# Gate products of a decoder kernel in four strips of 32 output partitions, summed by the product that turns them

## Chip, cores and metric

The kernel runs on one core of a Trainium2 chip. TensorE multiplies matrices (a float32 product is two records in a trace), VectorE, ScalarE and GpSimd work on elements, and SyncE issues most DMAs. The metric is the device time of one execution in microseconds, as the median over runs.

## What is computed

One decoder layer on x, 8 sequences of 256 tokens with 1024 features, all float32. It has three blocks, each behind a layernorm without weights, and each added to x:

```
x = x + attn(layernorm(x))               # 4 layers: scan over time, MLP 128 -> 512 -> 128
x = x + xattn(layernorm(x), ctx_4096)    # splits channels by top-k of ctx, gates both parts
x = x + ffn(layernorm(x))                # 8 experts, each token goes to its best two
...
gate_logits = jnp.einsum('bsh,he->bse', x, gate_w)        # x: (8, 256, 1024), gate_w: (1024, 8)
top_vals, top_idx = jax.lax.top_k(gate_logits, 2)
probs = jax.nn.softmax(top_vals, axis=-1)
expert_out = jnp.einsum('bsh,eho->bseo', x, expert_w)     # only of the chosen two in the kernel
```

The second block multiplies its input by a gate map, so the normed x before it (call it n1) times the map is what it adds. The change is about how `gate_logits` come about.

## The kernel before

The kernel is one program written out by hand: each engine has its own list, in program order, and waits on semaphores. No scheduler moves anything. It has these stages in time: the first block's four layers (to about 360 us); the stage in which x1 is made (`products`, `rows`), normed (`normed` on VectorE into `ring`), turned into feature-major tile T by TensorE (`turned`) and copied by ScalarE, while VectorE takes products and maxima over the channel groups (`crucial`, `maxima`, L1789 and L1798); the short serial stage of convolution and statistics (464 to 474 us: `band` products L1590 to L1595, filler products `keep_busy` L1603 of 512 bfloat16 columns that keep TensorE at work, sums over partitions L1607 and L1610, and a chain of small VectorE operations called `link`); the batch stage (474 to 530 us, 8 batches of 256 tokens); routing (to 561 us); and the loop over experts (L2099, from 563.64 us).

The logits of a token are found from two sums of products with gate_w, so that they don't wait for the whole second block. The first part, `first_part(c)` (c = 0 to 3, 512 tokens each), multiplies T before the gate map with the gate: eight products, one per block of 128 features, added up in one bank of the product memory, in its partitions 0 to 7. The second part, `second_part(b)` (b = 0 to 7, 256 tokens each), does the same with T after it was multiplied with the gate map. A sum is then copied by VectorE to `by_expert` (8 partitions wide; `first_sums` L1897, `second_sums` L1905) and turned to 128 tokens on partitions by 128x8 transposes (`first_turned` L1628, `second_turned` L1647), from where `known` and `logits` are made.

Where they stand in TensorE's list: `first_part(0)`, `first_part(1)` and the first half of `first_part(2)` behind the last turns of the x1 stage and ahead of the convolution; the second half of 2 and the first of 3 behind the statistics; the rest between `back(0)` and `first_turned(0)`. In the batch stage the order is `back(b)` (L1621: 16 transposes that turn the gated T back, for VectorE's `residual` L1877, which waits for each four), then `second_turned(b - 2)`, then `second_part(b)`; for b = 1, `first_turned(2)`, `first_turned(3)` and `second_part(0)` stand in the middle. VectorE's list for a batch is `residual(b)`, `behind(b - 1)` (L1891), `second_sums(b - 1)`, and the statistics of the new x. `back(b)` waits until `residual(b - 1)` has left its banks; `second_part(b)` waits for GpSimd's `gated_half` (L1472).

Of the kernel before, what the change touches and what calls it, by code (L numbers as in the profile page):

```python
# [8 lines left out]
U32 = mybir.dt.uint32  # L9
# [22 lines left out]
def crucial_count(c):  # L32
    f = int(LAMBDA * c // 1)
    return f + f % 2


def decoder_kernel(nc, x, ctx_map, w_in, b_in, ln1_w, ln1_b, phz_re, phz_im, lc_re, lc_im, sc_lin, ln2_w, ln2_b,
# [33 lines left out]
    with ctx:  # L71
# [26 lines left out]
        wout_t, bout_b = late[:, 0:D], late[:, D:2 * D]  # L98
        gate = sb("gate", [P, KD, E])
        convw = sb("convw", [P, 2 * TAPS])  # L100
# [47 lines left out]
        ld_misc = sem("ld_misc")  # L148
        ld_gate = sem("ld_gate")
        const_ready = sem("const_ready")  # L150
        set_pe = sem("set_pe")
# [230 lines left out]
        with nc.Block() as block:  # L382
            @block.sync
            def _(sp):
# [49 lines left out]
                context(3)  # L434
                sp.dma_start(gate[:, :, :], gate_w.rearrange("(k p) e -> p k e", p=P)).then_inc(ld_gate, 16)
                weights(2)
# [12 lines left out]
            def _(pool):  # L449
# [73 lines left out]
                def last_threshold(b):  # L523
# [12 lines left out]
                    chained(t2_set)  # L536

                g.memset(ident[:, :], 0.0).then_inc(const_ready, 1)
                g.memset(ones[:, :], 1.0).then_inc(const_ready, 1)
# [768 lines left out]
        pooled = ewide[:, 0:4 * KD * B].rearrange("p (m i k b) -> p m i k b", m=2, i=2, k=KD)  # L1308
        logits = sb("logits", [P, NT, E])
        totals = logits[:, :, :].rearrange("p t e -> p (t e)")[:, 0:KD * B].rearrange("p (k b) -> p k b", k=KD)  # L1310
# [12 lines left out]
        def pool_at(i, n):  # L1323
            b, h = divmod(n, CT)
            return pooled[:, 0, i, h * KU:(h + 1) * KU, b]

        def first_part(pe, c, first, last):

            if first == 0:
                pe.wait_ge(t_set, (c + 1) * KD * GROUP // S)  # L1330
                pe.wait_ge(x1_done, 2 * (NT - 2) + c + 1)
            for k in range(first, last):
                mm = nc.tensor.matmul(bank[P1_SUMS[c]][0:E, :], gate[:, k, :], T[:, k, c * GROUP:(c + 1) * GROUP], start=(k == 0), stop=(k == KD - 1))
            if last == KD:
                mm.then_inc(p1_mm, 1)
# [22 lines left out]
        std = in_late(NT)  # L1358
        g_part = in_late(E)
        known = in_late(NT, E)  # L1360
        shift = in_late(NT, E)
# [95 lines left out]
        P1 = N // GROUP  # L1457
        by_expert = [fin[0:E, u, :] for u in range(2)]

# [29 lines left out]
        col_s = [sb(f"col_s{u}", [P, QK], U32) for u in range(IN_FLIGHT)]  # L1489
        col_d = [sb(f"col_d{u}", [P, 1], U32) for u in range(IN_FLIGHT)]  # L1490
        col_p = [sb(f"col_p{u}", [P, 1]) for u in range(IN_FLIGHT)]
        xg_in = [sem(f"xg_in{u}") for u in range(IN_FLIGHT)]
# [10 lines left out]
        with nc.Block() as block:  # L1503
# [56 lines left out]
            def _(pe):  # L1560
# [63 lines left out]
                def first_turned(c):  # L1624
                    pe.wait_ge(p1_cp, c + 1)
                    for u in range(GROUP // P):
                        t = c * (GROUP // P) + u
                        mm = nc.tensor.transpose(bank[P1_BANK][:, t * E:(t + 1) * E], by_expert[c % 2][:, u * P:(u + 1) * P], ident[0:E, 0:E])  # L1628
                    mm.then_inc(p1_tp, 1)

                def second_part(b):

                    if b == 0:
                        pe.wait_ge(p1_cp, P1)
                    if b >= 2:
                        pe.wait_ge(p1_cp, P1 + b - 1)
                    for n in range(2):
                        wait_gated(pe, b, n)
                    for k in range(KD):
                        mm = nc.tensor.matmul(bank[P2_SUMS[b % 2]][0:E, 0:S], gate[:, k, :], T[:, k, b * S:(b + 1) * S], start=(k == 0), stop=(k == KD - 1))  # L1640
                    mm.then_inc(p1_mm, 1)

                def second_turned(b):
                    pe.wait_ge(p1_cp, P1 + b + 1)
                    for h in range(CT):
                        t = CT * b + h
                        mm = nc.tensor.transpose(bank[P2_BANK][:, t * E:(t + 1) * E], by_expert[b % 2][:, h * P:(h + 1) * P], ident[0:E, 0:E])  # L1647
                    mm.then_inc(l_mm, 1)
# [131 lines left out]
            def _(dve):  # L1780
# [68 lines left out]
                link(v.tensor_scalar(z[:, :, :], z[:, :, :], 0.0, None, ALU.max))  # L1849
                link(v.tensor_reduce(g_part, gate[:, :, :].rearrange("p k e -> p e k"), AX.X, ALU.add))  # L1850
                dve.wait_ge(g_act, 1)
# [41 lines left out]
                def first_sums(c):  # L1893
                    if c >= 2:
                        hold(dve, p1_tp, c - 1)
                    hold(dve, p1_mm, c + 1)
                    v.tensor_copy(by_expert[c % 2], bank[P1_SUMS[c]][0:E, :]).then_inc(p1_cp, 1)  # L1897

                def second_sums(b):
                    if b < 2:  # L1900
                        hold(dve, p1_tp, P1)
                    else:
                        hold(dve, l_mm, b - 1)
                    hold(dve, p1_mm, P1 + b + 1)
                    v.tensor_copy(by_expert[b % 2][:, 0:S], bank[P2_SUMS[b % 2]][0:E, 0:S]).then_inc(p1_cp, 1)  # L1905

# [315 lines left out]
```

## Time and profile before

| | us |
|---|---|
| median of 3 runs | 1089.44 (1087.9 to 1091.88) |
| the profiled execution | 1089.82 |
| its span, first to last instruction | 1087.9 |
| TensorE busy with products | 995.9 (92%) |
| VectorE busy | 538.7 (50%) |
| ScalarE, GpSimd busy | 383.5, 453.9 |
| mean granted TensorE clock | 0.955 of full speed |

Busy shares are means over stages with different bounds: the last 47% of the span belong to the expert products alone, and what lies before them must be read by stage. All times below count from the span's start.

### The profile page before, as it was taken

Reading aid. Unit: us, or ns where it says so; the run is one execution under the profiler, and the core shown is the slowest. Engines: PE = TensorE matmul, PEld = TensorE weight load, DVE = VectorE, ACT = ScalarE, POOL = GpSimd, SP = SyncE. Lnnn points to the kernel's source line nnn. Section 1 sums busy time; section 2 is a strip of 40 time slices with the busy share of each in tenths; the row PEclk is TensorE's granted clock in tenths of the full one; section 3 lists DMA queues with packets and bytes.
Section 4 is the critical chain, followed back from the end, with each engine's and each line's share of the span. In section 5 each row is a group of like instructions: output and inputs, shape, how many; then the busy total and the mean of one; then the engine's idle time right before and its main releaser. Section 6 shows DMA issues by size and latency. Waiting matters only on the chain. (4 is left out here: it accounts for less than half of the span.)

```text
span 1087.9 us, 13206 instructions
## 1 busy us (share of the span) xinstructions
PE 995.9 (92%) x3505; PEld 525.7 (48%) x3512; DVE 538.7 (50%) x1547; ACT 383.5 (35%) x1032; POOL 453.9 (42%) x567
## 2 busy tenths in 40 slices
PE   6888989999989799899469999999999999999995
PEld 5777555565555454245234444444444444444442
DVE  5645878999978889979952111111211111111111
ACT  2344868888865278668410000000000000000000
POOL 4823655665552010048244334333334444444441
PEclk9888989999989899899759999999999999999998
DMA  7320120110001330007758463737337364373332
GB/s 298 129 98 2 50 88 1 59 40 2 1 1 54 144 113 1 2 20 286 295 208 259 103 203 77 231 77 226 82 82 226 77 204 104 77 231 77 77 77 39
DMA packets 38461, 120.24 MB, mean 111 GB/s; under 512 B 6220, under 2 KB 9351, under 8 KB 38408
## 3 DMA queue, kind: packets, MB, share of 16 engines
q1 hardware_dynamic: 25592, 79.77, 19.8%
q0 software_dynamic: 12816, 39.86, 16.7%
q8 instruction: 21, 0.34, 0.1%
q14 instruction: 32, 0.26, 0.1%
HBM read 82.91 MB, written 36.70 MB: 110 GB/s over the span
## 5 line engine op out<-in xcount | busy, mean ns | idle before, releaser
L2099 PE MATMUL bank<-T,X 128*128 x1184 | 511.1, 595 | 3.7 <-issue 3.7
L2099 PEld LDWEIGHTS bank<-T,X 128*128 128x128 f32 x1184 | 225.9, 191 | 288.3 <-issue 288.3
L2144 DVE TENSOR_SCALAR X<-bank,col_p 128x512 f32<-128x512 f32 x37 | 27.8, 751 | 397.1 <-PE bank L2099 397.1
L2117 ACT ACTIVATE X<-bank,col_p 128x512 f32<-128x512 f32 x37 | 25.4, 687 | 495.8 <-PE bank L2099 469.7
L2062 POOL DMA_INDIRECT out_dram<-X,col_d x37 | 60.0, 1622 | 264.3 <-DVE X L2144 248.1
L2053 POOL DMA_INDIRECT X<-x_nrm,col_s x152 | 145.5, 957 | 50.8 <-issue 46.2
L850 ACT ACTIVATE M<-X,T 128x256 bf16<-128x256 f32 x152 | 75.0, 500 | 0.0
L490 POOL TENSOR_TENSOR rs<-ve,neg_half 128x4 f32<-128x4 f32 x36 | 43.7, 1214 | 57.9 <-DVE ve L978 57.9
L665 PE MATMUL bank<-nat,T 128*128 128x512 f32 x128 | 63.2, 614 | 2.5 <-ACT X L838 1.4
L1501 DVE STREAM_TRANSPOSE X<-X 128x1024 f32<-128x1024 f32 x39 | 48.4, 1240 | 26.3 <-DMA X<-x_nrm,col_s 12.7
L673 PE MATMUL bank<-X,T 128*128 128x512 f32 x128 | 60.6, 602 | 0.0
L607 PE MATMUL bank<-ident,rs 128*128 128x128 f32 x320 | 44.5, 285 | 16.4 <-POOL rs L490 14.2
L607 PEld LDWEIGHTS bank<-ident,rs 128*128 128x128 f32 x320 | 41.7, 195 | 36.5 <-POOL rs L490 23.0
L235 POOL TENSOR_TENSOR late<-late,neg_half 128x1 f32<-128x1 f32 x32 | 17.7, 556 | 93.3 <-DVE late L231 93.0
L838 ACT ACTIVATE X<-bank,T 128x512 f32<-128x512 f32 x64 | 43.5, 686 | 19.4 <-PE bank L665 17.9
L1009 DVE MAX8 T<-T 128x8 f32<-128x256 f32 x128 | 44.8, 412 | 0.1
L984 DVE TENSOR_TENSOR nat<-H,bank 128x512 f32<-128x512 f32 x36 | 24.5, 682 | 38.9 <-PE bank L607 38.5
L969 DVE TENSOR_TENSOR_SCAN X<-layer_par,X 128x256 f32<-128x256 f32 x64 | 42.7, 730 | 2.1 <-POOL X L494 2.0
L481 POOL TENSOR_TENSOR T<-T 128x8 f32<-128x8 f32 x88 | 38.2, 434 | 7.9 <-POOL T L481 1.4
L665 PEld LDWEIGHTS bank<-nat,T 128*128 128x128 f32 x128 | 21.7, 191 | 36.4 <-ACT X L838 21.8
L602 PEld LDWEIGHTS bank<-inv_col,nat 128*128 128x128 f32 x288 | 37.2, 202 | 2.6 <-ACT nat L825 2.2
L602 PE MATMUL bank<-inv_col,nat 128*128 128x1 f32 x288 | 37.1, 250 | 0.8 <-ACT nat L825 0.8
(341 smaller groups left out, 1426.6 us busy)
## 6 DMA issues: line engine op xcount, KB each, us to landing
T<-in_L_ffn_expert_w_dram SPq DMA_DIRECT2D x8, 4096.0 KB, 17.6
out_dram<-X SPq DMA_DIRECT2D x17, 512.0 KB
M<-in_x_dram SPq DMA_DIRECT2D x16, 512.0 KB, 7.2
X<-in_x_dram SPq DMA_DIRECT2D x16, 512.0 KB, 5.9
x_nrm<-H SPq DMA_DIRECT2D x16, 512.0 KB, 3.4
T<-in_ctx_dram SPq DMA_DIRECT2D x9, 512.0 KB, 3.7
X<-x_nrm,col_s POOLq DMA_INDIRECT x152
X<-in_ctx_dram SPq DMA_DIRECT2D x4, 512.0 KB, 7.0
```

What stands on the lines that cost most here:

```text
L490: g.tensor_tensor(rs[:, v % CH, :], ve[:, v % CH, :], neg_half[:, 0:TPC], ALU.pow).then_inc(done, 1)
L602: mm = nc.tensor.matmul(var_at(v, first)[:, i:i + 1], chunk(sq, v)[:, i * P:(i + 1) * P], inv_col[:, :], start=True, stop=True)
L607: mm = nc.tensor.matmul(bank[to][:, i * P:(i + 1) * P], rs[:, v % CH, i:i + 1].to_broadcast([P, P]), ident[:, :], start=True, stop=True)
L665: nc.tensor.matmul(bank[HD[t % 2]][:, :], w1s[v // CH % 2][:, t * P:(t + 1) * P], chunk(yn, v), start=True, stop=True).then_inc(hid_mm, 1)
L673: mm = nc.tensor.matmul(h_bank(v), w2c[v // CH % 2][:, t, :], hid[:, v % 2, t, :], start=False, stop=(t == FT - 1), skip_group_check=True)
L838: a.activation(hid[:, v % 2, t, :], bank[HD[t % 2]][:, :], ACT.Silu, bias=b1f[v // CH % 2][:, t:t + 1]).then_inc(hid_act, 1)
L850: a.activation(out_, tile_y(b, i), ACT.Sign, bias=at[b % 2][:, i:i + 1], accum_out=sums[b % 2][:, i:i + 1]).then_inc(done, 1)
L1009: v_.max(top16[b % 2][:, h * HT + i, r * 8:(r + 1) * 8], w[:, h, i, :]).then_inc(round_max, 1)
L1501: nc.vector.transpose(xgt_blocks[u], xg_blocks[u]).then_inc(xg_tp, 1)
L2053: g.indirect_dma_start(out=xg[u][:, c * QD:(c + 1) * QD], out_offset=None, in_=x_quarters, in_offset=bass.IndirectOffsetOnAxis(ap=col_s[u] ...
L2062: g.indirect_dma_start(out=out[:, :], out_offset=bass.IndirectOffsetOnAxis(ap=col_d[u][:, 0:1], axis=0), in_=yv[u], in_offset=None, comput ...
L2099: mm = nc.tensor.matmul(bank[2 * u + n][:, :], xgt[u][:, k, :], Tf[:, ds(odd * D + (k * N + n * BANK), BANK)], start=(k == 0), stop=(k == ...
```

## The change

The tile `gate` gets 32 columns per feature block in place of 8; the 24 new ones are zeroed by GpSimd at the start, and SyncE's load of the gate waits for that. Product k of a sum writes the partitions 32(k mod 4) to 32(k mod 4) + 31, so that four partial sums, of two feature blocks each, stand in four strips of a bank. The first four products of a sum start a strip, the last four close one. VectorE copies all 128 partitions. The turn becomes a float32 product: the copied block is the weight, and `sum_e`, a 128x8 matrix with a one in row 32j + e, column e, for j = 0 to 3, is multiplied with it; so it turns and adds the four strips at once. VectorE makes `sum_e` by one more reduction (of the identity) in the link chain ahead of L1850.

To make room, `logits` moves into the tile `center`, and `col_d` and `col_p` into the tiles `mv` and `ve`, which have no other use by then.

No instruction changes its place on any engine: GpSimd has one more (the zeroing, its first), VectorE one more (the reduction), and TensorE the same products in the same order.

```diff
-        gate = sb("gate", [P, KD, E])
+        gate = sb("gate", [P, KD, GROUP_E])
...
-                sp.dma_start(gate[:, :, :], gate_w.rearrange("(k p) e -> p k e", p=P)).then_inc(ld_gate, 16)
+                sp.wait_ge(gate_clear, 1)
+                sp.dma_start(gate[:, :, 0:E], gate_w.rearrange("(k p) e -> p k e", p=P)).then_inc(ld_gate, 16)
...
+                g.memset(gate[:, :, :], 0.0).then_inc(gate_clear, 1)
...
-        logits = sb("logits", [P, NT, E])
+        logits = center[:, :].rearrange("p (t e) -> p t e", e=E)
...
+        def of_group(sums, k):
+
+            j = k % GROUPS
+            return sums[j * GROUP_E:(j + 1) * GROUP_E, :]
...
-                mm = nc.tensor.matmul(bank[P1_SUMS[c]][0:E, :], gate[:, k, :], T[:, k, c * GROUP:(c + 1) * GROUP], start=(k == 0), stop=(k == KD - 1))
+                mm = nc.tensor.matmul(of_group(bank[P1_SUMS[c]], k), gate[:, k, :], T[:, k, c * GROUP:(c + 1) * GROUP], start=(k < GROUPS), stop=(k >= KD - GROUPS))
...
-        by_expert = [fin[0:E, u, :] for u in range(2)]
+        by_expert = [fin[:, u, :] for u in range(2)]
...
-        col_d = [sb(f"col_d{u}", [P, 1], U32) for u in range(IN_FLIGHT)]
-        col_p = [sb(f"col_p{u}", [P, 1]) for u in range(IN_FLIGHT)]
+        col_d = [mv[:, u, 0:1].bitcast(U32) for u in range(IN_FLIGHT)]
+        col_p = [ve[:, u, 0:1] for u in range(IN_FLIGHT)]
...
-                        mm = nc.tensor.transpose(bank[P1_BANK][:, t * E:(t + 1) * E], by_expert[c % 2][:, u * P:(u + 1) * P], ident[0:E, 0:E])
+                        mm = nc.tensor.matmul(bank[P1_BANK][:, t * E:(t + 1) * E], by_expert[c % 2][:, u * P:(u + 1) * P], sum_e[:, :], start=True, stop=True)
...
-                        mm = nc.tensor.matmul(bank[P2_SUMS[b % 2]][0:E, 0:S], gate[:, k, :], T[:, k, b * S:(b + 1) * S], start=(k == 0), stop=(k == KD - 1))
+                        mm = nc.tensor.matmul(of_group(bank[P2_SUMS[b % 2]], k)[:, 0:S], gate[:, k, :], T[:, k, b * S:(b + 1) * S], start=(k < GROUPS), stop=(k >= KD - GROUPS))
...
+                v.tensor_reduce(sum_e[:, :], ident[:, :].rearrange("p (j e) -> p e j", j=GROUPS)[:, 0:E, :], AX.X, ALU.add)
...
-                    v.tensor_copy(by_expert[c % 2], bank[P1_SUMS[c]][0:E, :]).then_inc(p1_cp, 1)
+                    v.tensor_copy(by_expert[c % 2], bank[P1_SUMS[c]][:, :]).then_inc(p1_cp, 1)
```

`GROUPS` is 4 and `GROUP_E` 32. The turn in `second_turned` and the copy in `second_sums` change in the same way.

## Rows read from the trace of the kernel before

**Rows 1.** The page's costliest groups: busy, mean ns | idle before, releaser

```profile
L2099 PE MATMUL bank<-T,X 128*128 x1184 | 511.1, 595 | 3.7 <-issue 3.7
```

**Rows 2.** Instructions on the tile gate: ns min/median/max, first and last start

```profile
L1640 PE MATMUL bank<-T,gate x128: 379/379/383, 486.1 to 526.8; 128*8 128x256 f32 x128
...
L1333 PE MATMUL bank<-T,gate x64: 592/592/1061, 442.7 to 482.2; 128*8 128x512 f32 x64
```

**Rows 3.** TensorE's timeline, 440 to 470 us: start, us, instruction [idle before <-releaser]

```profile
440.80 1.97 PE L1569 MATMUL bank<-ident,nat 128*128 128x128 f32 x8 [4.58 <-DVE nat L1806]
...
447.99 1.09 PE L1569 MATMUL bank<-ident,nat 128*128 128x128 f32 x8
...
453.56 10.47 PE L1333 MATMUL bank<-T,gate 128*8 128x512 f32 x24
464.87 0.71 PE L1590 MATMUL bank<-ewide,band 128*128 128x128 f32 x4 [0.84 <-DVE ewide L1826]
...
466.93 0.39 PE L1595 MATMUL bank<-ewide,band 128*128 128x56 f32 x2
467.15 1.46 PE L1603 MATMUL bank<-ones,ident 128*128 128x512 bf16 x6
468.44 0.28 PE L1607 MATMUL bank<-late,ones 128*128 128x2 f32 x2
...
470.03 0.38 PE L1610 MATMUL bank<-late,ones 128*128 128x2 f32 x2
```

**Rows 4.** VectorE's timeline in convolution and statistics, 464 to 473 us

```profile
464.52 0.30 DVE L1826 TENSOR_SCALAR ewide<-ewide 128x64 f32<-128x64 f32 x2
467.35 0.29 DVE L1837 COPY late<-bank 128x128 f32<-128x128 f32 x1 [2.53 <-PE bank L1595]
...
468.84 0.16 DVE L1840 TENSOR_SCALAR late<-bank 128x2 f32<-128x2 f32 x1 [0.88 <-PE bank L1607]
...
472.94 0.22 DVE L1853 TENSOR_TENSOR late<-late 128x64 f32<-128x64 f32 x1
```

**Rows 5.** Busy by stretch: PE, PEld, DVE, ACT, POOL, clock, DMA, GB/s

```profile
436.00:436.50 0.50, 0.22 (x2) 0.00 (x0) 0.50 (x5) 0.50 (x4) 0.00 (x0) 1.00 0.00 0
...
439.00:439.50 0.50, 0.00 (x0) 0.00 (x0) 0.50 (x3) 0.00 (x0) 0.00 (x0) 0.94 0.00 0
...
446.00:446.50 0.50, 0.50 (x2) 0.14 (x1) 0.50 (x2) 0.50 (x5) 0.00 (x0) 0.73 0.00 0
```

**Rows 6.** TensorE's timeline in the batch stage, 483 to 527 us

```profile
483.32 0.39 PE L1654 MATMUL bank<-late,ones 128*128 128x8 f32 x2
...
485.44 0.71 PE L1628 MATMUL bank<-ident,fin 8*128 8x8 f32 x8
486.08 7.07 PE L1640 MATMUL bank<-T,gate 128*8 128x256 f32 x32
493.08 1.97 PE L1621 MATMUL bank<-ident,T 128*128 128x128 f32 x16
494.98 0.29 PE L1647 MATMUL bank<-ident,fin 8*128 8x8 f32 x2
...
523.58 3.62 PE L1640 MATMUL bank<-T,gate 128*8 128x256 f32 x16
```

**Rows 7.** VectorE's timeline in the batch stage, 489 to 528 us

```profile
489.85 0.41 DVE L1905 COPY fin<-bank 8x256 f32<-8x256 f32 x1 [1.53 <-PE bank L1640]
...
501.42 2.48 DVE L1877 TENSOR_TENSOR X<-X,bank 128x512 f32<-128x512 f32 x4 [0.18 <-DVE late L1934]
...
507.96 2.48 DVE L1877 TENSOR_TENSOR X<-X,bank 128x512 f32<-128x512 f32 x4
...
527.53 0.40 DVE L1905 COPY fin<-bank 8x256 f32<-8x256 f32 x1
```

**Rows 8.** The timeline of the first microseconds: GpSimd's zeroing and TensorE's first product

```profile
0.99 0.43 POOL L540 MEMSET ewide<- 128x390 f32 x1
...
6.49 0.33 PE L744 MATMUL bank<-ident,T 59*128 59x59 f32 x1 [6.49 <-DMA T<-in_L_attn_lnl_b_dram]
```

More of the change, by code:

```diff
@@ L34, in crucial_count @@
     return f + f % 2
+GROUPS = 4
+GROUP_E = 128 // GROUPS
 def decoder_kernel(nc, x, ctx_map, w_in, b_in, ln1_w, ln1_b, phz_re, phz_im, lc_re, lc_im, sc_lin, ln2_w, ln2_b,
@@ L149, in decoder_kernel @@
         ld_gate = sem("ld_gate")
+        gate_clear = sem("gate_clear")
         const_ready = sem("const_ready")
@@ L1359, in decoder_kernel @@
         g_part = in_late(E)
+        sum_e = in_late(E)
         known = in_late(NT, E)
@@ L1646, in second_turned @@
                         t = CT * b + h
-                        mm = nc.tensor.transpose(bank[P2_BANK][:, t * E:(t + 1) * E], by_expert[b % 2][:, h * P:(h + 1) * P], ident[0:E, 0:E])
+                        mm = nc.tensor.matmul(bank[P2_BANK][:, t * E:(t + 1) * E], by_expert[b % 2][:, h * P:(h + 1) * P], sum_e[:, :], start=True, stop=True)
                     mm.then_inc(l_mm, 1)
@@ L1849, in _ @@
                 link(v.tensor_scalar(z[:, :, :], z[:, :, :], 0.0, None, ALU.max))
-                link(v.tensor_reduce(g_part, gate[:, :, :].rearrange("p k e -> p e k"), AX.X, ALU.add))
+                v.tensor_reduce(sum_e[:, :], ident[:, :].rearrange("p (j e) -> p e j", j=GROUPS)[:, 0:E, :], AX.X, ALU.add)
+                link(v.tensor_reduce(g_part, gate[:, :, 0:E].rearrange("p k e -> p e k"), AX.X, ALU.add))
                 dve.wait_ge(g_act, 1)
@@ L1904, in second_sums @@
                     hold(dve, p1_mm, P1 + b + 1)
-                    v.tensor_copy(by_expert[b % 2][:, 0:S], bank[P2_SUMS[b % 2]][0:E, 0:S]).then_inc(p1_cp, 1)
+                    v.tensor_copy(by_expert[b % 2][:, 0:S], bank[P2_SUMS[b % 2]][:, 0:S]).then_inc(p1_cp, 1)
                 for k in range(KU):
```

## The prediction

> **What bounds the kernel now.** I first read the chain that ended last and the table of costly groups. The routed expert products (L2099) are 1184 matmul records, 511.1 us of a span of 1087.9 [rows 1]. They start at 563.64 us and the change does not touch them, so what it can win or lose must lie before that moment. I then looked for the gate products by line: L1333 (first part, 32 products of 128x512 in 64 records) and L1640 (second part, 64 products of 128x256 in 128 records) [rows 2]. A float32 product is two records. Their starts are the measure of their cost, since a record's own length has a tail that overlaps the next. At L1333 24 records took 10.47 us, 0.43 us a record, 0.86 a product; at L1640 32 took 7.07 us, 0.22 a record, 0.43 a product [rows 3, 6]. So the gate products hold TensorE for 32 x 0.86 + 64 x 0.43 = 55 us.
>
> The third view, the timeline of two engines side by side, tells what those 55 us are worth. Before 464.87 us TensorE runs L1333 while VectorE does the channel sums, and the next TensorE step, the convolution L1590, starts when VectorE has done L1826 (464.52 + 0.30 = 464.82), 0.84 us after TensorE fell idle [rows 3, 4]. TensorE is no bound there. In the batch stage (478 to 528 us) TensorE looks full: per batch 16 back-turns (1.90 us from 493.08 to 494.98), two logit turns (0.2) and a second part (3.62 with its tail), 5.7 us together. But VectorE takes 6.54 us a batch (501.42 to 507.96) and does not wait [rows 6, 7]. There VectorE is the bound and TensorE is ahead of it. The one place where VectorE waits for a gate product is the copy of the second part of batch 0: 1.53 us at 489.85 [rows 7]. It is the only stall in the trace that faster gate products can take away.
>
> **What the change does to the products.** The eight products of a sum now write four strips of 32 partitions in turn (k modulo 4), and each still is two records. The trace of before has no two products in different strips, so their overlap has to be bounded. At one end nothing overlaps: 0.86 us a 512-column product. At the other end four run at once: 0.22. I take a middle: the second record of a product needs the strip of its first, so it starts 0.43 us after it; the first record of the next product, in another strip, can run beside it; if records start in program order, as every row here shows them, a stream then moves one product per record time. That is 0.43 us per 512-column product and 0.22 per 256-column one, half of before.
>
> The Trainium skill ("TensorE: Matmul & The Clock Gate", Part 3: Packing small matmuls) says that products in different column strips run at the same time and that matmuls start and end in program order. No row here shows the first; the second agrees with every row. The same part says that weight loads pass running matmuls only where the row group differs, which is not so for column strips, and by it little overlap would be left: that is the third case below.
>
> **Convolution and statistics (the largest term).** L1333 there is 12 products, now 10.47 us from 453.56. At half the time they end at about 453.56 + 12 x 0.43 + 0.43 = 459.1. The convolution still waits for VectorE until 464.87, so TensorE idles 5.7 us instead of 0.84. What an idle stretch does to its clock is in the trace: its last work before 440.80 ended at 436.2, and the granted clock was down to half in the half microsecond from 439.0 [rows 5]: 3.2 us later. It is at half (1.2 instead of 2.4 GHz) at 440.80, where eight transposes took 1.97 us against 1.09 at the full clock [rows 3], and comes back at 446.25 (0.73 in the half from 446.0), 5.4 us after work resumed. So after the change the clock falls at about 462.3, the convolution starts at half clock, and full clock returns near 464.87 + 5.4 = 470.3. The 20 convolution records took 2.28 us (464.87 to 467.15); at half clock about 4.5, to 469.4. Behind them stand six filler products of 512 bf16 columns, 1.29 us to L1607 (468.44); of these 0.9 us run at half clock and the rest at full: they end at about 471.1 and L1607 is 2.7 us late. VectorE sat idle for each of these steps (2.53 us before L1837, 0.88 before L1840) [rows 4], so the delay is on the path. The second filler group then runs at full clock and adds nothing. Term: **+2.7 us**. Its ends: 0 where the clock holds; 4.7 where the clock stays at half through both fillers (2.2 + 1.3 + 1.2).
>
> **The stall at 489.85.** The turn of a sum was a transpose, one record; it is now a float32 product with the strip-adding matrix, two records. The nearest product of that shape, L1654, took 0.39 us for its two records, and 16 records with as many weight columns took 1.97 in a row, so 0.1 us for each record more [rows 6]. The turns of the third and fourth 512-column sums (8 records, 0.71 us at 485.44) get 8 more: 0.8 us. The second part of batch 0 then starts at 486.9 instead of 486.08, takes 8 x 0.22 + 0.22 = 1.9 instead of 3.45, and ends near 488.9 instead of 489.6. The copy goes 0.7 us earlier: **-0.7 us**. Ends: -1.5 (the whole stall, if four overlap), +0.8 (no overlap). Behind that, VectorE's 6.54 us a batch stay the bound: TensorE needs 1.97 + 0.5 + 1.9 = 4.4.
>
> **Small edits.** The new reduction of the identity on VectorE sits in the serial gate chain between L1849 and L1853 and is read from 32 numbers a partition; small VectorE operations here take 0.15 to 0.22, the last of them L1853 [rows 4]: **+0.15 us** (0 if wholly under the sigmoid, 0.3 at most). The zeroing of the gate tile is 256 numbers a partition, under the 0.43 us of L540 with 390; it delays GpSimd's constants by 0.3 us at 1 us, and TensorE's first step waits for a DMA until 6.49 [rows 8]: 0, and 0.3 without that cover. SyncE's new wait for it is passed a hundred microseconds later. The copies read 128 partitions instead of 8 at equal width; 8x256 took 0.41, and four operations of 128x512 from the same kind of tile 2.48, 0.6 each [rows 7], so a width of 256 on all partitions costs no more than that: 0. The new homes of logits, col_d and col_p move nothing. The gate load is one DMA that lands hundreds of microseconds early: 0. All else keeps its order.
>
> **Sum.** 2.7 - 0.7 + 0.15 = +2.15 us on the profiled execution's 1089.8 (span 1087.9 and 1.9 around it): 1092.0. The median of the runs is 0.4 under that execution, so 1091.6. All that follows is against the median, 1089.4.
>
> **The rivals.**
> *The clock holds.* The overlap is as above, but TensorE's idle stretch doesn't meet the throttle, or VectorE's steps before it end sooner: -0.7 + 0.15, 1088.9. For it: the stretch is only 2.5 us longer than the 3.2 after which it fell. Against it: it did fall there.
> *No overlap: the change doesn't do what it says.* The products take what they took, and only the longer turns remain. VectorE's copy waits 0.8 us longer at 489.85. Then TensorE, at 5.7 + 0.2 a batch, stays under 6.54 at first, but the last three batches of VectorE come closer, and its last copy at 527.53 follows TensorE's last second part (from 523.58 for 3.62 us) closely [rows 6, 7]. That part would end 0.8 + 6 x 0.22 = 2.1 us later, the copy about 1.9 later: 1089.4 + 1.9 + 0.15 = 1091.4. No clock is lost.
> *All four strips at once.* The products take a quarter. The stall goes wholly (-1.5), TensorE idles from 456.8 to 464.87, so the half clock is certain: +2.7. Together +1.35: 1090.8. The Trainium skill ("TensorEngine Tiling (Array Packing)", Overview) gives up to 4x for 32 columns; no run here shows it.
> *Slower beyond doubt: half clock in the batch stage.* If four overlap, TensorE works 1.97 + 0.5 + 1.0 = 3.5 of 6.54 us a batch and the gap is 3.1 us, near the 3.2 after which the clock fell. At half clock a batch is 7 to 9 us of TensorE and it becomes the bound; without a gap it then wins the clock back after some 5.4 us, so about every second of six batches loses 2.3 us: +7 on top of the forecast's 2.15, 1098.5. It decides from a gap of about 3.2 us on; at my rate the gap is 2.1, which is against it.
>
> **How the numbers follow.** Forecast (pairs overlap, cold convolution) 0.42; clock holds 0.18; no overlap 0.20; four at once 0.13; half clock in the batches 0.07. The predicted time is 1091.6. The first four cases lie between 1088.9 and 1091.6; with the bounds of the clock term (4.7 instead of 2.7: 1093.6), the third bound of the stall, and the spread of the runs before (1087.9 to 1091.9) the range is 1087.5 to 1094.5. Half a percent is 5.4 us, about what a measurement of this kernel can tell from no change: to a time under 1084.0 none of these cases leads, and 0.02 stands for what I don't see; over 1094.9 the last case and a little of the clock's tail, 0.08; within, 0.90.
>
> **What would show it.** In the profile after: L1333's and L1640's records in starts per product (0.43 and 0.22 right, 0.86 and 0.43 no overlap, less for four); TensorE idle for 5 us before the convolution and a granted clock of 0.50 at 465 us; the convolution's 20 records over 4 us; VectorE's waits for them up by 2 to 3 us; the wait before the batch 0 copy at about 0.8; VectorE still at 6.5 us a batch with the clock at 1.00; the expert loop at 511 us. The forecast fails if the products don't overlap, if the granted clock stays at 1.00 at 465 us, or if VectorE waits for TensorE in the batches.

## The result, and the profile of the changed kernel

The changed kernel takes 1093.2 us (median of 20 runs, 1089.14 to 1097.17) against 1089.09 (20 runs, 1087.08 to 1092.27). The ratio is 1.0031, with a 95% interval of 1.0019 to 1.0043: slower by 0.3%, less than the half percent that the prediction names, with a median 1.6 us above the forecast. Its profiled span is 1091.9 us (before 1087.9) and its mean granted clock 0.936 (before 0.955).

The expert loop is the same, one line of the page's costliest groups, to be read beside [rows 1]:

```profile
L2113 PE MATMUL bank<-T,X 128*128 x1184 | 511.0, 595 | 4.0 <-issue 4.0
```

So the 4.0 us lie before it. TensorE's timeline of the changed kernel from the last first-part products ahead of the convolution to the second part of batch 0 (start, us, instruction, idle before and its releaser) answers to [rows 3, 6]; lines have moved by 12 to 14, so L1345 is the old L1333, L1603 the old L1590, L1653 the old L1640, L1641 the old L1628, and L1634 the old L1621:

```profile
453.99 4.25 PE L1345 MATMUL bank<-T,gate 128*32 128x512 f32 x24
465.76 1.23 PE L1603 MATMUL bank<-ewide,band 128*128 128x128 f32 x4 [7.52 <-DVE ewide L1839]
...
470.07 2.77 PE L1616 MATMUL bank<-ones,ident 128*128 128x512 bf16 x6
472.63 0.43 PE L1620 MATMUL bank<-late,ones 128*128 128x2 f32 x2
...
474.76 0.28 PE L1623 MATMUL bank<-late,ones 128*128 128x2 f32 x2
474.97 1.92 PE L1345 MATMUL bank<-T,gate 128*32 128x512 f32 x16
...
485.32 1.95 PE L1641 MATMUL bank<-late,fin 128*128 128x8 f32 x16
...
487.36 3.33 PE L1634 MATMUL bank<-ident,T 128*128 128x128 f32 x16
490.48 2.17 PE L1641 MATMUL bank<-late,fin 128*128 128x8 f32 x16
492.57 1.93 PE L1653 MATMUL bank<-T,gate 128*32 128x256 f32 x32
```

Sixteen records of L1345 take 1.92 us at the full clock, 0.12 each, 0.24 a product, where [rows 3] had 0.86. The second part's 32 records take 1.93 instead of 7.07 [rows 6]. From the first start of L1653 to the start of the work behind it the 32 records hold TensorE for 1.87 us (492.57 to 494.44) where they held it for 7.00: by a factor of 3.7 less, close to a quarter and not half. (The 24 records from 453.99 took 4.25 us, more than 24 times 0.12, because the granted clock was at half from 453.6 to 457.0.) In front of the convolution TensorE is now idle for 7.52 us instead of 0.84.

VectorE's timeline of the changed kernel in the same stretch and three batches on, which answers to [rows 4, 7]:

```profile
465.41 0.29 DVE L1839 TENSOR_SCALAR ewide<-ewide 128x64 f32<-128x64 f32 x2
470.32 0.29 DVE L1850 COPY late<-bank 128x128 f32<-128x128 f32 x1 [4.61 <-PE bank L1608]
...
473.17 0.16 DVE L1853 TENSOR_SCALAR late<-bank 128x2 f32<-128x2 f32 x1 [2.24 <-PE bank L1620]
...
475.15 0.16 DVE L1858 TENSOR_SCALAR late<-bank 128x2 f32<-128x2 f32 x1 [0.85 <-PE bank L1623]
...
477.58 0.22 DVE L1867 TENSOR_TENSOR late<-late 128x64 f32<-128x64 f32 x1
...
493.82 0.42 DVE L1919 COPY fin<-bank 128x256 f32<-128x256 f32 x1 [0.84 <-PE bank L1653]
...
505.50 2.48 DVE L1891 TENSOR_TENSOR X<-X,bank 128x512 f32<-128x512 f32 x4 [0.18 <-DVE late L1948]
...
512.06 2.48 DVE L1891 TENSOR_TENSOR X<-X,bank 128x512 f32<-128x512 f32 x4
```

The three waits for TensorE in convolution and statistics have grown from 2.53, 0.88 and 0.55 to 4.61, 2.24 and 0.85. The third one before stood in this line:

```profile
470.52 0.16 DVE L1845 TENSOR_SCALAR late<-bank 128x2 f32<-128x2 f32 x1 [0.55 <-PE bank L1610]
```

The reason stands in the view by stretch (busy of PE, PEld, DVE, ACT, POOL, then the granted clock, DMA share, GB/s), first of the kernel before, then of the changed kernel:

```profile
467.00:474.00 7.00, 7.00 (x28) 2.57 (x28) 3.92 (x15) 1.01 (x3) 0.70 (x1) 1.00 0.00 0
```

```profile
464.00:466.00 2.00, 0.24 (x1) 0.24 (x2) 1.41 (x9) 1.08 (x1) 0.00 (x0) 0.50 0.00 0
...
472.00:474.00 2.00, 2.00 (x7) 1.03 (x6) 0.74 (x3) 0.00 (x0) 0.00 (x0) 0.50 0.00 0
474.00:476.00 2.00, 2.00 (x18) 0.99 (x20) 0.45 (x2) 0.00 (x0) 0.61 (x1) 0.98 0.00 0
...
505.00:511.00 6.00, 4.66 (x25) 4.44 (x29) 5.61 (x14) 4.55 (x7) 5.85 (x6) 0.50 0.60 235
```

Both of the chip's levels are there: 0.50 is 1.2 GHz, 1.00 is 2.4. In the kernel before, the same stage ran at 1.00 throughout. In the changed one TensorE's last product ended at 458.24 and the granted clock fell at 460.4. The convolution, the first sum over partitions and most of the fillers now run at half clock, and the clock comes back at 474.1 us, 8.3 us after TensorE took up work. It also fell for times in the batch stage: from 480.9 to 484.3 and from 487.8 to 491.2, which bears on the stall of batch 0 (below), and again from 504.8 on, as the last row shows, where it cost nothing.

Taken stage by stage between VectorE's own marks, the 4.0 us come together like this:

| stretch | before | after | difference |
|---|---|---|---|
| start of span to convolution input (L1826, now L1839) | 464.52 | 465.41 | +0.89 |
| to the copy of its result | 2.83 | 4.91 | +2.08 |
| to the mean | 1.49 | 2.85 | +1.36 |
| to the variance | 1.68 | 1.98 | +0.30 |
| to the difference of the averages (L1853, now L1867) | 2.42 | 2.43 | 0.0 |
| to the copy of batch 0 | 16.91 | 16.24 | -0.67 |
| to the start of the loop | 73.79 | 73.92 | +0.13 |
| loop and end | 524.3 | 524.2 | -0.1 |

The first row is not the change's. In twelve profiled runs of this study, the place where the convolution's input is ready lies between 462.4 and 467.2 us (5.8 us of added copies taken off in one), in kernels with strips in the first part (462.9, 464.3, 465.2, 465.4, 467.0, 467.2) as in those without (462.4, 462.5, 464.5, 465.0, 465.4, 466.7). One place where the two profiles part is in the first block: near 100 us the clock was at half for some 3 us in the kernel before (from 98.1) and for some 7 in the changed one (from 105.4), and TensorE's work is 1 us later behind it. Differences of a microsecond between two profiles are therefore read by stage, and those between kernels from the medians.

### The profile page after: what moved, and what is told of

Same layout as the page of the kernel before. It is cut to its first block and busy times, and to the rows that moved or that the text cites. A ratio compares the mean times of both kernels' runs of the same rounds, so it can differ in the third digit from the quotient of the medians.

```text
span 1091.9 us, 13272 instructions
## 1 busy us (share of the span) xinstructions
PE 974.4 (89%) x3537; PEld 531.9 (49%) x3544; DVE 539.2 (49%) x1548; ACT 383.7 (35%) x1032; POOL 455.2 (42%) x568
## 5 line engine op out<-in xcount | busy, mean ns | idle before, releaser
L2158 DVE TENSOR_SCALAR X<-bank,ve 128x512 f32<-128x512 f32 x37 | 27.8, 751 | 394.8 <-PE bank L2113 394.8
L2131 ACT ACTIVATE X<-bank,ve 128x512 f32<-128x512 f32 x37 | 25.4, 687 | 495.4 <-PE bank L2113 495.4
L2076 POOL DMA_INDIRECT out_dram<-X,mv x37 | 60.0, 1622 | 263.9 <-DVE X L2158 247.7
```

The costliest lines, as they stand in the source:

```text
L2076: g.indirect_dma_start(out=out[:, :], out_offset=bass.IndirectOffsetOnAxis(ap=col_d[u][:, 0:1], axis=0), in_=yv[u], in_offset=None, comput ...
```

## The experiments

The theory after the result: (A) the first part's saving is worth nothing, since VectorE bounds TensorE there, and its idle stretch costs the clock in the serial stage, some 3.7 us; (B) the second part's saving is worth up to the 1.53 us stall of batch 0, and the longer turns take back about half. The rivals: the strips cost something by themselves, or the wider gate and the longer turns do; and for the overlap: pairs, or all four strips.

**e1_fill: filler products ahead of the convolution.** The changed kernel with `keep_busy` defined earlier and

```diff
+                pe.wait_ge(t_set, KD * B)
+                keep_busy(7, 24)
```

in TensorE's list between the first-part products and the convolution.

> The changed kernel with 24 filler products of 512 bfloat16 columns on TensorE between the last first-part product and the convolution (5.2 us at the full clock), nothing else. Clock theory (the loss is the convolution and statistics at half clock, behind an idle stretch of 7.5 us that the faster products left): the granted clock is 1.00 at the convolution, its 20 records take 2.3 us again instead of 4.3, VectorE's two waits fall from 4.6 and 2.2 us to 2.5 and 0.9, and the time falls by 3.4 to 3.8 us from the changed kernel's, to a ratio of 0.999 to 1.000 to the kernel before. Rival (the longer turns and wider copies in the batches cost it): the time stays at 1.003.

Measured: 1089.94 us (12 runs) against 1090.17, ratio 1.0001 (0.9987 to 1.0014). The loss of 0.31% is gone from the medians. But the profiled execution missed part of what was expected. TensorE's timeline of e1_fill:

```profile
455.62 5.35 PE L1606 MATMUL bank<-ones,ident 128*128 128x512 bf16 x24
463.21 0.71 PE L1612 MATMUL bank<-ewide,band 128*128 128x128 f32 x4 [2.23 <-DVE ewide L1841]
...
464.99 0.63 PE L1617 MATMUL bank<-ewide,band 128*128 128x56 f32 x2
```

The fillers ended 2.23 us early, and from 464.7 us on the clock was at half in this execution (0.63 instead of 0.39 us for two records of 56 columns), in the middle of the work. So the clock fell here behind a gap of 2.2 us, too. VectorE's three waits were 3.35, 2.25 and 1.43 us, 3.07 more than before, so this execution kept most of the 3.75 us that it should have won back, against the expected waits of 2.5 and 0.9. That its time (1090.5 us) lies near that of the kernel before comes from an early start: its convolution's input was ready at 462.9. The medians agree with (A), but this profile does not show it, and e1 alone is no proof.

**e8_fill_both: enough fillers, at both gaps.** As e1_fill, with

```diff
-                keep_busy(7, 24)
+                keep_busy(7, 34)
...
+                keep_busy(7, 16)
```

the second group behind the products at 472.8 us, ahead of `back(0)`.

> The changed kernel with 34 filler products ahead of the convolution (7.3 us at full clock, up to VectorE's last sums) and 16 in the idle stretch of 3.9 us between the statistics and the first back-turns. Clock theory: granted clock 1.00 from 457 us to the batches, VectorE's waits in convolution and statistics 2.5 to 2.9, 0.9 and 0.5 us, and the stall at the copy of batch 0's second part smaller than 0.8; ratio 0.998 to 0.999. Rival (the fillers themselves delay the path): waits over 3 us at a clock of 1.00.

Measured: 1089.43 us (11 runs) against 1090.33, ratio 0.9984 (0.9969 to 0.9999). VectorE's timeline first and then TensorE's, of e8_fill_both:

```profile
469.83 0.29 DVE L1853 COPY late<-bank 128x128 f32<-128x128 f32 x1 [2.53 <-PE bank L1617]
...
471.32 0.16 DVE L1856 TENSOR_SCALAR late<-bank 128x2 f32<-128x2 f32 x1 [0.88 <-PE bank L1622]
...
491.65 0.43 DVE L1922 COPY fin<-bank 128x256 f32<-128x256 f32 x1 [0.82 <-PE bank L1656]
```

```profile
459.81 7.51 PE L1606 MATMUL bank<-ones,ident 128*128 128x512 bf16 x34
...
487.65 1.95 PE L1644 MATMUL bank<-late,fin 128*128 128x8 f32 x16 [1.90 <-DVE fin L1914]
489.54 3.61 PE L1656 MATMUL bank<-T,gate 128*32 128x256 f32 x32
```

With TensorE at work the waits are 2.53 and 0.88 to the hundredth as in [rows 4], the third is 0.55, and the granted clock was 1.00 from 458.9 to 489.5. The whole +3.75 is the clock's. The stall of batch 0 stayed at 0.82, where less had been expected: the turns had to wait for VectorE's copy of the sums, then took 1.95 us, and the products of batch 0 behind them ran at half clock (32 records in 3.61 us instead of 1.93), which is as much again as the stall.

**e5_idle: the same gap without any strip.** The kernel before, with work put into VectorE's list ahead of the averages:

```diff
+                for i in range(8):
+                    v.tensor_copy(ring[1], X[:, 0, :]).then_inc(extra, 1)
+                    dve.wait_ge(extra, i + 1)
```

> The kernel before, with eight copies of 1024 columns on VectorE (about 7 us of empty work) between its last channel maxima and the averages, so that TensorE idles some 8 us ahead of the convolution with no strips anywhere. Clock theory: the convolution takes 4.3 us instead of 2.3, VectorE's waits there grow to 4.6 and 2.2 us as in the changed kernel, and the time grows by the copies plus 3.5 to 3.8 us. Rival (strips or the 32-column gate slow the convolution): the waits stay at 2.5 and 0.9 us and only the copies are added.

Measured: 1100.52 us (4 runs) against 1090.33, ratio 1.0076 (1.0053 to 1.0099). TensorE and VectorE of e5_idle:

```profile
471.17 1.22 PE L1591 MATMUL bank<-ewide,band 128*128 128x128 f32 x4 [6.82 <-DVE ewide L1830]
```

```profile
475.72 0.29 DVE L1841 COPY late<-bank 128x128 f32<-128x128 f32 x1 [4.61 <-PE bank L1596]
...
478.58 0.16 DVE L1844 TENSOR_SCALAR late<-bank 128x2 f32<-128x2 f32 x1 [2.25 <-PE bank L1608]
...
481.08 0.16 DVE L1849 TENSOR_SCALAR late<-bank 128x2 f32<-128x2 f32 x1 [1.38 <-PE bank L1611]
```

The copies took 5.8 us (not the 7 I had counted on) and the gap was 6.8 (not 8). The waits of 4.61 and 2.25 are those of the changed kernel, in a kernel whose products are the old ones; the third is 1.38, since the clock came back only at 480.6, 9.4 us after work resumed. The half clock follows the gap, not the strips. From the convolution's input to the difference of the averages the stage is 4.3 us longer, and with 5.8 us of copies that is 10.1, what the medians say (10.2; the ratio of four runs says 8.3, with an interval from 5.8 to 10.8).

**e2_second_only: strips in the second part alone.** The first part goes to one strip of 32 partitions, and its turn is a product with the first 32 rows of `sum_e`:

```diff
-                mm = nc.tensor.matmul(of_group(bank[P1_SUMS[c]], k), gate[:, k, :], T[:, k, c * GROUP:(c + 1) * GROUP], start=(k < GROUPS), stop=(k >= KD - GROUPS))
+                mm = nc.tensor.matmul(bank[P1_SUMS[c]][0:GROUP_E, :], gate[:, k, :], T[:, k, c * GROUP:(c + 1) * GROUP], start=(k == 0), stop=(k == KD - 1))
```

> Strips in the second part alone; the first part sums in one strip of 32 and is turned by a product over 32 partitions. Clock theory: the first part again fills TensorE up to the convolution, so no loss there (VectorE's waits 2.5 and 0.9 us), and the second part's gain at the one stall stays (1.5 us down to 0.8 or less): ratio 0.999 to 1.000. Rival (strips cost time in themselves, by switching, or the turns cost it): slower than before, 1.001 to 1.003.

Measured: 1089.04 us (12 runs) against 1090.17, ratio 0.9999 (0.9984 to 1.0014). TensorE and VectorE of e2_second_only:

```profile
484.73 1.95 PE L1641 MATMUL bank<-late,fin 32*128 32x8 f32 x16
486.61 1.93 PE L1653 MATMUL bank<-T,gate 128*32 128x256 f32 x32
```

```profile
487.86 0.42 DVE L1919 COPY fin<-bank 128x256 f32<-128x256 f32 x1 [1.49 <-PE bank L1653]
```

No clock is lost, since TensorE has its old amount of work ahead of the convolution: VectorE's waits there are 2.53, 0.88 and 0.55. But the stall is 1.49, as long as before and not 0.8 as expected: what the second part wins, the turns take away. There are two groups of them ahead of that copy, each 16 records in 1.95 us where 8 transposes took 0.66 and 0.71 ([rows 6] has the second). I had priced only one of the groups.

**e3_first_only: strips in the first part alone.** The second part in one strip, by the same kind of edit.

> Strips in the first part alone; the second part in one strip, turned by a product. Clock theory: the convolution is at half clock again, plus 3.5 to 4 us, and the stall at the copy of batch 0's second part is not shortened but lengthened, 1.5 to over 2 us: ratio 1.003 to 1.005. Rival (the batch stage carries the loss): 1.000 to 1.001.

Measured: 1096.45 us (6 runs), ratio 1.0060 (1.0043 to 1.0078). VectorE of e3_first_only:

```profile
470.07 0.29 DVE L1850 COPY late<-bank 128x128 f32<-128x128 f32 x1 [4.61 <-PE bank L1608]
...
495.31 0.41 DVE L1919 COPY fin<-bank 32x256 f32<-32x256 f32 x1 [2.50 <-PE bank L1653]
```

The clock is lost and the stall grows by 0.97. The time is above the expected 1.003 to 1.005: VectorE's last copy of the batch stage waits 1.53 us for TensorE, which had not been counted. With 3.8 from the clock these make 6.3 us, as the medians do. The longer turns are in this run too; against e4_one_strip (next), which has the turns and no strips, strips in the first part shorten the stall from 4.03 to 2.50 and lose 3.8 us by the clock, so by themselves they cost more than they bring.

**e4_one_strip: no strips at all, all else of the change.** Both parts in one strip: the gate's width, the wider copies' place, the turns as products and the new reduction remain.

> No strips: both parts sum in one strip of 32 columns, everything else of the change stays (wider gate tile, zeroing, product turns, extra reduction, moved tiles). It is the case of no overlap of the prediction, which gave +1.9 and +0.15 us: ratio 1.0015 to 1.002, with the last copies of VectorE waiting for TensorE about 2 us. Clock theory: no clock loss at the convolution. If the gate width of 32 costs TensorE time, a product of 512 columns takes over 0.86 us.

Measured: 1093.81 us (12 runs) against 1090.17, ratio 1.0034 (1.0021 to 1.0048). TensorE and VectorE of e4_one_strip:

```profile
468.16 7.05 PE L1345 MATMUL bank<-T,gate 128*32 128x512 f32 x16
...
486.46 7.09 PE L1653 MATMUL bank<-T,gate 128*32 128x256 f32 x32
```

```profile
490.25 0.41 DVE L1919 COPY fin<-bank 32x256 f32<-32x256 f32 x1 [4.03 <-PE bank L1653]
...
529.74 0.41 DVE L1919 COPY fin<-bank 32x256 f32<-32x256 f32 x1 [1.53 <-PE bank L1653]
```

With 32 columns of weights instead of 8 a product takes as long as before (7.05 us for 16 records of 512 columns, 7.03 before; 7.09 for 32 of 256, 7.07 in [rows 6]), so the width is free. The clock holds in the convolution. The stall is 4.03, 2.5 more than 1.53: two groups of turns, each 1.25 longer. Another 1.53 us appear as a wait before the last copy of the batch stage. This is the prediction's second rival carried out, and it costs 3.7 us by the ratio (3.6 between the medians), not 2.05 (1.9 and 0.15).

**e6_two_strips: two strips instead of four.** One run.

```diff
-            j = k % GROUPS
+            j = k % 2
```

with start and stop to match, and copies and turns of 64 partitions.

> The changed kernel with two strips (k modulo 2) in place of four. If a product in another strip starts beside the one before at no cost, the products of 512 columns take 0.43 us each at full clock, 0.22 for 256 columns, twice what four strips take. If overlap was limited by the pair of records of a product, as the prediction had it, two strips would take the same as four.

Measured: 1092.77 us. TensorE of e6_two_strips:

```profile
473.88 3.63 PE L1345 MATMUL bank<-T,gate 128*32 128x512 f32 x16
...
490.92 3.65 PE L1653 MATMUL bank<-T,gate 128*32 128x256 f32 x32
```

Two strips take 3.63 of one strip's 7.05 us, four 1.92: the time goes down nearly in proportion to the strips, and two strips don't take the same as four.

**e7_adjacent: four strips, neighbouring products in the same one.** One run.

```diff
-            j = k % GROUPS
+            j = k // 2
```

> The changed kernel with the blocks dealt to the strips in neighbours (blocks 0 and 1 to strip 0, 2 and 3 to strip 1, and so on) in place of one after the other in turn; the same products, turns and sum. It tells whether four strips overlap because neighbouring products lie in different strips, or because later products may pass earlier ones. If a product waits for the one ahead of it in its own strip and the products behind it wait too (order kept), then only products of different pairs overlap, and of every two products about one is hidden: the eight gate products of the first part take between 0.43 and 0.65 us each, against 0.24 in the changed kernel and 0.87 with one strip, so they are no quicker than with two strips. If products may pass one another, 0.22 to 0.24 us a product, as in the changed kernel. Convolution and averages run at the half clock in both cases; the span lies between 1088 and 1094 us.

Measured: 1093.83 us. TensorE of e7_adjacent:

```profile
476.88 1.94 PE L1345 MATMUL bank<-T,gate 128*32 128x512 f32 x16
```

As fast as with alternating strips. If a product held up all that stand behind it until its strip is free, this would have taken two to three times as long. In this kernel as in the changed one the view by tenths of a microsecond has four of these records in progress at a time (eight where one four follows another). Which of two explanations holds, that records of another strip start ahead of a waiting one or that some queue behind the start takes them in, these rows don't tell, because they don't name the strip of a record.

The profile shows one thing more. The work is the same as in the changed kernel, but VectorE doesn't wait at the copy of batch 0:

```profile
494.94 0.42 DVE L1919 COPY fin<-bank 128x256 f32<-128x256 f32 x1
```

Here the granted clock was 1.00 from 486.4 on, and the stretch from the difference of the averages to this copy is 15.45 us (16.24 in the changed kernel, 16.91 before). In the changed kernel's profile the clock was at half from 487.8 to 491.2. So the 0.84 us that were left of the stall there come from the clock, too, and not from the turns alone.

**e9_mixed and e10_mixed_again: the version the runs point to.** Strips in the second part alone, as e2_second_only, but the first part exactly as in the kernel before: 8 partitions, and transposes of one record.

```diff
-                        mm = nc.tensor.matmul(bank[P1_BANK][:, t * E:(t + 1) * E], by_expert[c % 2][0:GROUP_E, u * P:(u + 1) * P], sum_e[0:GROUP_E, :], start=True, stop=True)
+                        mm = nc.tensor.transpose(bank[P1_BANK][:, t * E:(t + 1) * E], by_expert[c % 2][0:E, u * P:(u + 1) * P], ident[0:E, 0:E])
```

> Strips in the second part alone, and the first part exactly as in the kernel before: 8 partitions wide, turned by one-record transposes. If the longer turns ate the gain of the second part in the run with strips in the second part alone, that gain comes back here: the second part of batch 0 ends 2.4 us earlier than before, so VectorE's 1.5 us wait at its copy is gone, the convolution is untouched, ratio 0.9985 to 0.999. Rival (the stall has another cause, such as the gated tiles of GpSimd): the wait stays near 1.5 and the ratio at 1.000.

Measured: 1087.43 us (12 runs, 1084.58 to 1089.58) against 1090.33 (23 runs), ratio 0.9965 (0.9952 to 0.9978). TensorE and VectorE of e9_mixed:

```profile
487.60 0.72 PE L1641 MATMUL bank<-ident,fin 8*128 8x8 f32 x8
488.24 1.93 PE L1653 MATMUL bank<-T,gate 128*32 128x256 f32 x32
```

```profile
475.10 0.22 DVE L1867 TENSOR_TENSOR late<-late 128x64 f32<-128x64 f32 x1
...
490.41 0.40 DVE L1919 COPY fin<-bank 128x256 f32<-128x256 f32 x1
```

The wait before the copy is gone, and the stretch from the difference of the averages to it is 15.3 us instead of 16.91: -1.6. The time is lower than the expected ratio of 0.9985 to 0.999; 1.3 us of the medians' 2.9 were unexplained, so the same kernel was run once more.

> The kernel of e9_mixed word for word, once more. Its profile accounts for 1.5 us less than before from the convolution on, its times for 2.9. If the stages tell the whole, the ratio comes out at 0.9986, with an interval that holds it; if the stages before the convolution are really shorter in most executions, the ratio is again near 0.9965 and a second profile may begin the convolution before 464.5 us, where the kernel before did (e9_mixed: 466.7). In both cases no wait before the batch 0 copy, 1.5 to 1.7 us less from the difference of the averages to that copy, and convolution and averages as in the kernel before.

Measured: 1086.21 us (12 runs) against 1089.48 (17 runs), ratio 0.9970 (0.9957 to 0.9983), so the 0.9986 lies outside the interval. The stretch is 15.31 again, the convolution's input ready at 465.42, no earlier than before, so in the profile the stages ahead are not the rest either. It is in the loop: the pages of the two give

```profile
L2113 PE MATMUL bank<-T,X 128*128 x1184 | 510.1, 594 | 4.4 <-issue 4.4
```

and 510.0 for the same records, where [rows 1] has 511.1. The view by stretch of the kernel before, whose loop begins at 563.64, and then of e9_mixed, whose loop begins at 564.34:

```profile
568.00:570.00 2.00, 2.00 (x5) 0.94 (x4) 0.00 (x0) 0.00 (x0) 1.40 (x2) 0.71 1.03 404
```

```profile
566.00:568.00 2.00, 2.00 (x4) 0.81 (x3) 0.00 (x0) 0.00 (x0) 1.39 (x3) 0.55 1.01 391
568.00:570.00 2.00, 2.00 (x7) 0.81 (x6) 0.00 (x0) 0.00 (x0) 1.59 (x2) 1.00 1.00 389
```

The loop of e9_mixed runs at half clock for its first 3.5 us, that of e10_mixed_again for 3.3, that of the kernel before (563.64 to 569.2) for 5.5. A microsecond less at half clock is worth half a microsecond here: 2.0 and 2.2 us less, and a loop shorter by 1.0 and 1.1. With -1.6 that makes -2.6 to -2.7, near the medians' -2.9 and -3.3. Why the clock is back sooner in both profiles isn't shown. It is no mark of this version: the loop took 509.8 us in e7_adjacent, where the clock was back after 3.0 us, and 510.7 to 511.3 in the other profiles. So 1.6 us are shown to be the edit's; the other microsecond was there in both profiles and has no known cause.

## Why the prediction was right or wrong

The sign was right and the time within the range, 1.6 us above the forecast. Three steps were not right: how products in strips overlap, when the clock comes back, and what the turns cost. The first and the third cancelled in the stall, and that was luck.

**How products in strips overlap: wrong.** The step that failed is "if records start in program order [...] a stream then moves one product per record time". Which of its two conditions failed, the order of the starts or a record's wait for the one ahead of it in its strip, is not shown. Four strips gave 0.24 us a product and not 0.43 (the changed kernel), two gave 0.45 (e6_two_strips), and the deal among the strips doesn't matter (e7_adjacent: 0.24). The case "all four strips at once" holds, which I had at 0.13. It is the one that the Trainium skill ("TensorEngine Tiling (Array Packing)", Overview) states, up to 4x for 32 columns: here 0.87 to 0.24 us. The other rule of the Trainium skill that I had weighed, from "TensorE: Matmul & The Clock Gate", Part 3: Packing small matmuls, that weight loads pass running products only where the row group differs, did not limit anything: all records here use all rows, and their time fell to little over a quarter.

**Convolution and statistics: mechanism right, term too small.** +2.7 was forecast, +3.75 measured, inside the stated ends of 0 and 4.7. The convolution's 20 records took 4.31 us (465.76 to 470.07) for the 4.5 I had. What was off is the clock's return: I took over 5.4 us from the one precedent in the trace and had it back at 470.3, ahead of most of the fillers. It came back at 474.1, 8.3 us after work resumed, and in e5_idle some 9.4 us after. So the first fillers cost 1.3 more instead of 0.4 and the second group another 0.4. One precedent is no constant. The same holds for the fall: the prediction had 3.2 us from the end of work to the half clock, and here it was 2.2 (458.24 to 460.4). e8_fill_both shows that nothing but the clock is in this term.

**Stall of batch 0: right size by luck.** -0.7 forecast, -0.67 measured. The products saved more than I had: from 4.03 in e4_one_strip to 1.49 in e2_second_only, which is 2.54 instead of 1.55. The turns cost more. I had priced one of the two groups ahead of that copy, at 0.8, with 0.1 us for a record where the row that I read gives 0.12 (1.97 for 16); both groups count, at 1.25 each at full clock. Two groups at 1.25 on top of 1.53 make 4.03, which is e4_one_strip's stall. In the changed kernel the first part's last products, ahead of the first turns, are quicker too, and the half clock takes part of that back, which the forecast had at nothing here. Counted by starts on TensorE, which doesn't pause between the back-turns of batch 0 and that copy:

| step | before | after | difference |
|---|---|---|---|
| difference of the averages to the back-turns of batch 0 | 4.37 | 3.20 | -1.17 |
| these back-turns | 1.89 | 3.55 | +1.66 |
| last products of the first part | 3.53 | 0.99 | -2.54 |
| first group of turns | 0.59 | 1.81 | +1.22 |
| to the end of the back-turns of batch 1 | 2.12 | 3.35 | +1.23 |
| second group of turns | 0.64 | 2.09 | +1.45 |
| second part of batch 0 | 3.50 | 0.94 | -2.56 |

The sum is -0.7. Some 3.1 us of the rises are the half clock's (both back-turns and the first records of the second group). Without it the stall would have gone wholly, as the rival with all four strips at once had it, and as it did in e7_adjacent, where the back-turns of batch 1 took 1.94 us and not 3.33.

**The small edits: nothing.** The new reduction takes 0.20 us, but the stretch that holds it is 2.43 against 2.42 us long: VectorE's next reduction starts 0.12 us later and the chain absorbs it. The wider gate and the copies from 128 partitions (0.42 us, 0.41 before) cost nothing, as forecast. Nor does the zeroing: TensorE's first product waits for the same DMA in all profiles, to 6.49 us in the kernel before and to 6.49 to 6.67 in the kernels with the zeroing.

**Batch stage: right, and closer to the rival than thought.** VectorE keeps 6.56 us a batch (505.50 to 512.06), against 6.54. The half clock did come: 0.50 from 505 to 511 us. I had said that it decides from a TensorE gap of 3.2 us; the gap was 3.86, but gaps of 2.11 us (before 452.80) and of 2.23 (e1_fill) were enough elsewhere, so that figure is no bound. What the rival had wrong is the price. This batch took TensorE 5.8 us from start to end, 506.34 to 512.1, under VectorE's 6.56, with the clock back at 511.7. Wholly at half clock it would be about 6.1 by my estimate: 3.44 for the back-turns (506.34 to 509.78), 0.79 for the turns, and 1.87 for the products, twice their 0.94. I had put it at 7 to 9, twice the sums of 3.5 and 4.4, which count the records' tails.

**No overlap: priced too low.** 1091.4 stood for it, +2.05. e4_one_strip is that case, and costs 3.7 us, for the same reason as above: only one group of turns had been counted. The turns of each later batch also cost 0.33 us more instead of 0.22 (four records in 0.54 where two took 0.21), and so the last copy waits.

By the ratio the change costs 3.4 us (2.1 to 4.7), between the medians 4.1. The stages of the profile give +3.75 and -0.67, which is 3.1.

## What to carry to other kernels

Ask of every stage that you make faster what its engine does with the time. Ahead of a serial stage in which TensorE is waited for, idle time can be worth less than nothing: here the 20 products ahead of the convolution became 12 us shorter together, which bought 3.75 us of loss, and filler products that reached up to the convolution took that loss back. Where a packed form needs a costlier step to gather its result, use it only where its saving is on the path: strips in the second part alone, with the old cheap turn elsewhere, took 0.3% less time than the kernel before and some 0.6% less than the changed one.

## What the runs showed of the hardware

Float32 products of 32 output partitions in different column strips overlap with little loss: sixteen records of 512 columns take 7.05 us in one strip, 3.63 in two, 1.92 in four, whether neighbours share a strip or not (1.94). Products with 8 and with 32 weight columns take the same (7.03 and 7.05 us). A turn of a 128-column block by a float32 product costs two records of 0.12 us, a transpose of 8 partitions one of 0.08. The granted clock, once at half, came back 5.4, 8.3 and 9.4 us after work resumed in three stretches (the kernel before, the changed one, e5_idle). It also fell while TensorE was at work, shortly behind a gap: about 0.8 us after it had resumed from a gap of 2.11 us (changed kernel, 453.6), 1.5 us after one of 2.23 (e1_fill, 464.7), 1.9 us after one of 1.90 (e8_fill_both, 489.5).
